# First query and output projections as three split fp32r products from one reloaded weight home

## What is computed

```python
h = layernorm(x)
q, k, v = h @ Wq, ctx @ Wk, ctx @ Wv              # 16 heads of 32
x = x + softmax(q k^T / sqrt(512 / 16), masked by len) v @ Wo
h = layernorm(x)
idx, gates = softmax_of_top2(relu(mean_over_tokens(h) @ gw1.T + gb1) @ gw2.T + gb2)   # 8 experts
proj_p(y) = y @ Wm_p.T + sum_k gates_k * ((y @ V_p[idx_k].T) * S_p[idx_k]) @ U_p[idx_k] + b_p   # rank 16
x = x + proj_o(softmax(proj_q(h) / sqrt(32) proj_k(h)^T) proj_v(h))
```

## Time and profile before

| | |
|---|---|
| median of 3 runs | 1458.2 us (1456.44 to 1459.19) |
| the profiled execution's own time | 1457.15 us |
| its span | 1455.3 us, 16992 instructions |
| TensorE busy | 1396.1 us, 96%, granted clock 0.965 |
| VectorE, ScalarE, GpSimd busy | 952.3 (65%), 862.4 (59%), 681.0 us (47%) |
| DMA | 130.81 MB, mean 90 GB/s |

### The profile page before, as it was taken

The page is one execution under the profiler, slowest core; times in us unless marked ns, Lnnn a source line. Parts: engine busy times, 40 slices in busy tenths (PEclk is TensorE's granted clock), DMA queues, the critical chain, the costliest instruction groups (busy, mean ns, idle before and its releaser), DMA issues.

```text
span 1455.3 us, 16992 instructions
## 1 busy us (share of the span) xinstructions
PE 1396.1 (96%) x5624; PEld 697.0 (48%) x5624; DVE 952.3 (65%) x1687; ACT 862.4 (59%) x1499; POOL 681.0 (47%) x411
## 2 busy tenths in 40 slices
PE   6998999999999999999999999999999999899886
PEld 4534444554455454554455554555455554444332
DVE  4364467766767677766767677766767676766632
ACT  2426364865567663866577663866577663756441
POOL 2021143546556362546556362546546362567463
PEclk9878998999999999999999999999999999999968
DMA  6533123532334224532334224531434222422210
GB/s 209 157 104 98 45 59 101 136 89 45 90 110 110 74 52 123 140 84 45 95 105 111 74 52 123 141 83 45 98 102 111 74 52 81 131 59 54 71 34 29
DMA packets 78239, 130.81 MB, mean 90 GB/s; under 512 B 26358, under 2 KB 31094, under 8 KB 75079
## 3 DMA queue, kind: packets, MB, share of 16 engines
q1 hardware_dynamic: 74055, 128.66, 33.0%
q10 hardware_dynamic: 4096, 1.06, 0.3%
HBM read 66.08 MB, written 12.21 MB: 54 GB/s over the span
## 4 chain that ended last, share of the span: by engine, by line
PE 87%; ACT 6%; issue 2%; DMA 2%; POOL 1%; DVE 1%; SPq 1%; ACTq 0%; POOLq 0%; DVEq 0%
PE pj L1091 44%; PE scT L1176 9%; PE acc L1205 8%; PE sc L1148 8%; PE sc L1137 4%; PE pj L1121 2%; PE pj L1185 2%; PE scT L1169 2%; PE pj L1193 2%; PE pj L1214 2%; PE pj L1085 2%; ACT xhat L705 2%; PE pj L1066 1%; ACT qs L788 1%; PE pj L1077 1%
## 5 line engine op out<-in xcount | busy, mean ns | idle before, releaser
L820 ACT ACTIVATE probs<-scT 128x512 f32<-128x512 f32 x512 | 289.2, 594 | 314.5 <-PE scT L1176 310.5
L936 DVE TENSOR_REDUCE negmax<-sc 128x1 f32<-128x512 f32 x512 | 338.0, 684 | 149.9 <-PE sc L1148 149.1
L683 POOL TENSOR_TENSOR probs_sum<-probs_sum,probs 128x1024 f32<-128x1024 f32 x128 | 300.0, 2368 | 61.5 <-ACT probs L820 61.5
L1148 PE MATMUL sc<-ks,qs 96*128 96x512 f32 x512 | 263.3, 549 | 6.6 <-DMA ks<-ks 3.1
L963 DVE RECIPROCAL inv_sum<-pj 128x128 f32<-128x128 f32 x256 | 224.9, 921 | 64.5 <-PE pj L1214 44.5
L1176 PE MATMUL scT<-qs,ks 99*128 99x512 f32 x512 | 254.7, 526 | 8.5 <-ACT probs L820 5.6
L1091 PE MATMUL pj<-XT,Wqk 128*128 128x512 f32 x512 | 259.6, 603 | 0.0
L679 POOL TENSOR_TENSOR probs_sum<-probs 128x1024 f32<-128x1024 f32 x64 | 151.5, 2373 | 194.2 <-ACT probs L820 194.2
L1176 PEld LDWEIGHTS scT<-qs,ks 99*128 99x128 f32 x512 | 97.2, 196 | 130.2 <-ACT probs L820 62.3
L689 POOL TENSOR_TENSOR uv_stack<-UVS_sb,uv_stack 96x1024 fp32r<-96x1024 f32 x32 | 75.7, 2364 | 171.9 <-ACT UVS_sb L727 171.9
L653 POOL TENSOR_TENSOR xhat<-xhat,inv_sum 128x128 f32<-128x128 f32 (+1 forms) x56 | 46.7, 833 | 212.6 <-DVE inv_sum L963 212.6
(11 more groups left out here) (99 smaller groups left out, 1710.1 us busy)
## 6 DMA issues: line engine op xcount, KB each, us to landing
Wqk<-in_WmT SPq DMA_DIRECT2D x16, 1024.0 KB, 6.5
Wvo<-in_WmT SPq DMA_DIRECT2D x16, 1024.0 KB, 5.7
UVS_sb<-in_UVS SPq DMA_DIRECT2D x64, 192.8 KB, 3.2
qs<-stage_lo SPq DMA_DIRECT2D x136, 64.0 KB, 2.3
qs<-qs SPq DMA_DIRECT2D x34, 256.0 KB, 3.0
X<-in_x SPq DMA_DIRECT2D x8, 1024.0 KB, 5.8
ks<-stage_lo SPq DMA_DIRECT2D x128, 64.0 KB, 2.0
ks<-ks SPq DMA_DIRECT2D x32, 256.0 KB, 3.0
```

The costliest lines, as they stand in the source:

```text
L683: nc.gpsimd.tensor_tensor(probs_sum[:, pair], probs_sum[:, pair], probs[:, kt % 2, pair], ALU.add)\
L820: nc.scalar.activation(probs[:, kt % 2, jj, :], scT[:, ST[step], :], ACT.Exp, scale=SCALE)\
L936: nc.vector.tensor_reduce(negmax[:, 0, n:n + 1], sc[:, SC[step], :], AX.X, ALU.max, negate=True)\
L1148: nc.tensor.matmul(sc[:, SC[step], :], qs[0:3 * DH, slot, jj, t * P:(t + 1) * P], ks[0:3 * DH, slot, jj, :], start=True, stop=True).then_i ...
```

## The change

1. **Split products.** Each of the 16 `q1` and 16 `out1` products of a batch becomes three products on fp32r operands that add up in the same bank: high weight x high data, high x low, low x high. `product` takes a list of terms.
2. **One home for both weights.** `W1` holds the high and low part of one 512x512 weight, 2 MB. `w1_split` makes both parts of both weights once, at the start, and stores them in DRAM (`w1_hbm`). From batch 1 on `w1_load` brings Wq's parts after the last `out1` of the batch before, and Wo's after the last `q1`.
3. **Splitting the data.** For `q1`, `xpose` of the first half writes its copy as `hi1` (ScalarE), and VectorE subtracts it from the bank into `lo1`. For `out1`, new steps `c_hi` (ScalarE) and `c_lo` (GpSimd) split each quotient of `cdivide` into the same `hi1` and `lo1`.
4. **Transposes by feature block.** An `xpose` step takes one block of 128 features from all four token tiles, not all features of one tile. The second half's step writes `XT[:, c]`; `token_sums` reduces one feature block straight into `pooled`.
5. **Room.** `STAGES` is 2. `gw1T` and the loaded U and V live in `probs1`, S in `S_sb`, and `vb` and `ob` share `bias_sb`; `gw1_load`, `vb_load` and `ob_load` bring them in every batch, on SyncE's queue, and `csT` waits until `uv_lo` has read U and V.
6. **Calendar.** The period stays; nearly all due times in `CALENDAR` and `OWN` are written anew. Between `gate_hidden` and the first `weff`, ScalarE's order is now: two exps of `sT`, `qk_split`, two exps, an `xpose` copy, `gate_scale`, a copy, an exp, two copies, two `qk_rows`, `uv_hi`; `normalize` of the next batch stands ahead of `gate_hidden`. TensorE's order there holds 14 matmuls of `sc` and `sT`, 7 `q1`, 4 `xpose`, 2 `pv`, a `den`, a `shift` and `gate_top`. `uv_lo` of the last OP pair stands ahead of the last divides, and `residual_bias` moves from a due time of 1404 to one of 2289. Column-tiled runs number 20 in a period, 162 in the kernel.

```diff
+UV_ROWS, UV_COLS = 2 * 3 * R, 2 * D
-STAGES = 3
+STAGES = 2
...
-        UVS_sb = sb("UVS_sb", [UV_ROWS, 2, UV_COLS])
+        W1 = sb("W1", [P, 2, DC, D], F32R)
+        S_sb = sb("S_sb", [UV_ROWS, 2, 4])
-        gw1T_sb = sb("gw1T_sb", [P, DC, P])
-        vb_sb = sb("vb_sb", [P, D])
-        ob_sb = sb("ob_sb", [P, D])
+        bias_sb = sb("bias_sb", [P, D])
+        lo1 = sb("lo1", [P, DC, S], F32R)
+        hi1 = sb("hi1", [P, DC, S], F32R)
...
+        gw1T_sb = probs1[:].rearrange("p j n -> p (j n)")[:, 0:D].rearrange("p (c n) -> p c n", c=DC)
+        UV_sb = probs1[0:UV_ROWS].rearrange("p j n -> p (j n)").rearrange("p (a n) -> p a n", a=2)
...
-        carrier = sb("carrier", [P, 1])
-
-
-        early = XT[:, 1].rearrange("p c n -> p (c n)")
+        carrier = sb("carrier", [P, 3])
+
+
+        early = probs[:].rearrange("p a j n -> p (a j n)")[:, DC * B * NK:DC * B * NK + 2 * P]
+        first_raw = Wqk[:, 0], ctx2T[:]
...
+                if p == QP:
+                    sp.wait_ge("w1_lo", sp.after("w1_lo", "w1_split", 0))
...
+            def w1_split(step, w):
+                sp.wait_ge("w1_hi", sp.after("w1_hi", *step))
+                sp.wait_ge("w1_lo", sp.after("w1_lo", *step))
+                queue.dma_start(w1_hbm[w], W1[:].bitcast(F32)).then_inc(sems[f"w1_stored{w}"], 16)
+
+            def w1_load(step, b, w):
+                if b == 0:
+                    return
+                if w:
+                    for i in range(DC):
+                        sp.wait_ge("pj_full", sp.after("pj_full", "q1", b, i, DC - 1))
+                else:
+                    for t in range(TT):
+                        sp.wait_ge("pj_full", sp.after("pj_full", "out1", b - 1, t, DC - 1))
+                for part in range(2):
+                    sp.wait_ge(f"w1_stored{part}", sp.after(f"w1_stored{part}", "w1_split", part))
+                queue.dma_start(W1[:].bitcast(F32), w1_hbm[w]).then_inc(sems["w1_loaded"], 16)
+
+            def gw1_load(step, b):
+                sp.wait_ge("pj_full", max(sp.after("pj_full", "cpv", b, DC - 1), sp.after("pj_full", "cden", b, DC - 1)))
+                for p in (QP, KP, VP):
+                    sp.wait_ge("uv_split", sp.after("uv_split", "uv_lo", b - 1, p))
+                queue.dma_start(gw1T_sb, gw1T.rearrange("(c p) n -> p c n", p=P)).then_inc(sems["gw1_loaded"], 16)
+
+            def vb_load(step, b):
+                sp.wait_ge("bias_added", sp.after("bias_added", "residual_bias", b - 1))
+                queue.dma_start(bias_sb[:], vb.rearrange("(a n) -> a n", a=1).to_broadcast([P, D]))\
+                     .then_inc(sems["vb_loaded"], 16)
+
+            def ob_load(step, b):
+                sp.wait_ge("pj_left_by_dve", max(sp.after("pj_left_by_dve", "v_bias", b, t) for t in range(TT)))
+                queue.dma_start(bias_sb[:], ob.rearrange("(a n) -> a n", a=1).to_broadcast([P, D]))\
+                     .then_inc(sems["ob_loaded"], 16)
+
+                if b >= 2:
+                    sp.wait_ge("uv_scaled", sp.after("uv_scaled", "uv_hi", b - 2, OP))
+                for k in range(2):
+                    rows = Ss[bass.ds(chosen[b][k], 1)].rearrange("a r p -> (a r) p")
+                    queue.dma_start(S_sb[k * 3 * R:(k + 1) * 3 * R, b % 2, :], rows).then_inc(sems["s_loaded"], 16)
+                crossed = min(b + 1, B - 1) if p == OP else b
+                sp.wait_ge("pj_full", sp.after("pj_full", "gate_hidden", crossed))
+                sp.wait_ge("pj_full", max(sp.after("pj_full", "cpv", crossed, DC - 1), sp.after("pj_full", "cden", crossed, DC - 1)))
-                    queue.dma_start(UVS_sb[k * 3 * R:(k + 1) * 3 * R, n, :], rows).then_inc(sems[f"uv_loaded{n}"], 16)
+                    queue.dma_start(UV_sb[k * 3 * R:(k + 1) * 3 * R, n, :], rows).then_inc(sems[f"uv_loaded{n}"], 16)
...
+            def c_lo(step, b, i, piece):
+                n = S // pieces(i)
+                at = slice(piece * n, (piece + 1) * n)
+                pool.wait_ge("c_hi", pool.after("c_hi", "c_hi", b, i, piece))
+                nc.gpsimd.tensor_tensor(lo1[:, i, at], ctx1T[:, i, at], hi1[:, i, at].bitcast(F32), ALU.subtract)\
+                    .then_inc(sems["c_split"], 1)
+
+            pool.walk({"c_lo": c_lo, "uv_lo": uv_lo, "deviation": deviation, "cdivide": cdivide,
...
-            def xpose(step, b, half, t):
-                if half == 0:
-                    act.wait_ge("pj_full", max(act.after("pj_full", "qk", b - 2, DC - 1, w, DC - 1) for w in range(2)))
+            def xpose(step, b, half, c):
+                if half:
+                    act.wait_ge("pj_full", max(act.after("pj_full", "v", b - 2, t, DC - 1) for t in range(TT)))
+                    act.wait_ge("pj_full", max(act.after("pj_full", "qk", b - 2, j, w, DC - 1) for j in JOBS for w in range(2)))
+                else:
+                    act.wait_ge("pj_full", max(act.after("pj_full", "out1", b - 1, t, DC - 1) for t in range(TT)))
-                nc.scalar.activation(XT[:, b % 2, :, t * P:(t + 1) * P],
-                                     pj[:, PJ[step], :].rearrange("p (c n) -> p c n", c=DC), ACT.Copy)\
-                    .then_inc(sems["pj_left_by_act"], 1)
+                dst, done = (XT[:, b % 2, c, :], "pj_left_by_act") if half else \
+                    (hi1[:, c, :], "xt_hi")
+                nc.scalar.activation(dst, pj[:, PJ[step], :], ACT.Copy).then_inc(sems[done], 1)
+
+            def w1_split(step, w):
+                act.wait_ge(("wq1_loaded", "wo1_loaded")[w], 16)
+                if w:
+                    for i in range(DC):
+                        act.wait_ge("pj_full", act.after("pj_full", "q1", 0, i, DC - 1))
+                    act.wait_ge("w1_stored0", act.after("w1_stored0", "w1_split", 0))
+                nc.scalar.activation(W1[:, 0], first_raw[w], ACT.Copy).then_inc(sems["w1_hi"], 1)
+
+            def c_hi(step, b, i, piece):
+                n = S // pieces(i)
+                at = slice(piece * n, (piece + 1) * n)
+                for k in range(DC):
+                    act.wait_ge("pj_full", act.after("pj_full", "q1", b, k, DC - 1))
+                act.wait_ge("normed", act.after("normed", "cdivide", b, i, piece))
+                nc.scalar.activation(hi1[:, i, at], ctx1T[:, i, at], ACT.Copy).then_inc(sems["c_hi"], 1)
...
+                if j == 0 and i == 0:
+                    for p in (QP, KP, VP):
+                        act.wait_ge("uv_split", act.after("uv_split", "uv_lo", b - 1, p))
+                    act.wait_ge("uv_split", act.after("uv_split", "uv_lo", b - 2, OP))
...
+            def xpose(step, b, half, c):
+                if half:
+                    return
+                for k in range(TT):
+                    dve.wait_ge("pj_full", dve.after("pj_full", "out1", b - 1, k, DC - 1))
+                dve.wait_ge("xt_hi", dve.after("xt_hi", *step))
+                nc.vector.tensor_tensor(lo1[:, c, :], pj[:, PJ[step], :], hi1[:, c, :].bitcast(F32), ALU.subtract)\
+                    .then_inc(sems["pj_left_by_dve"], 1)
+
+            def w1_split(step, w):
+                dve.wait_ge("w1_hi", dve.after("w1_hi", *step))
+                nc.vector.tensor_tensor(W1[:, 1], first_raw[w], W1[:, 0].bitcast(F32), ALU.subtract)\
+                    .then_inc(sems["w1_lo"], 1)
...
-            def token_sums(step, b, t):
-                dve.wait_ge("pj_left_by_act", dve.after("pj_left_by_act", "xpose", b, 1, t))
-                nc.vector.tensor_reduce(tile_sums[:, :, t:t + 1], XT[:, b % 2, :, t * P:(t + 1) * P], AX.X, ALU.add)\
+            def token_sums(step, b, c):
+                dve.wait_ge("pj_left_by_act", dve.after("pj_left_by_act", "xpose", b, 1, c))
+                nc.vector.tensor_reduce(pooled[:, c:c + 1], XT[:, b % 2, c, :], AX.X, ALU.add)\
-                if t == TT - 1:
-                    dve.wait_ge("gate_step", dve.after("gate_step", *step, k=1))
-                    nc.vector.tensor_reduce(pooled[:], tile_sums[:], AX.X, ALU.add).then_inc(sems["gate_step"], 1)
...
-            def xpose(step, b, half, t):
+            def xpose(step, b, half, c):
-                pe.wait_ge("xhat_done", pe.after("xhat_done", "normalize", b, half, k=t + 1))
-                for dc in range(DC):
-                    mm = nc.tensor.transpose(pj[:, p, dc * P:(dc + 1) * P], xhat[:, t, dc * P:(dc + 1) * P], ident_sb[:])
+                pe.wait_ge("xhat_done", pe.after("xhat_done", "normalize", b, half))
+                for t in range(TT):
+                    mm = nc.tensor.transpose(pj[:, p, t * P:(t + 1) * P], xhat[:, t, c * P:(c + 1) * P], ident_sb[:])
-            def product(step, name, lhsT, rhs, dc):
+            def product(step, name, terms, dc):
-                mm = nc.tensor.matmul(pj[:, p, :], lhsT, rhs, start=(dc == 0), stop=(dc == DC - 1))
+                for n, (lhsT, rhs) in enumerate(terms):
+                    mm = nc.tensor.matmul(pj[:, p, :], lhsT, rhs, start=(dc == 0 and n == 0),
```

(31 more changed lines are left out.)

279 lines of the change are left out of this document (153 added, 126 removed), and 54 rows, old and new, of tables (CALENDAR, OWN).

## The result

The changed kernel takes 1482.65 us (median of 4 runs, 1477.85 to 1485.67) against 1458.68 us, a ratio of 1.0169 with a 95% interval of 1.0136 to 1.0202. It is 1.7% slower where I forecast 0.6% faster, and outside my range.

What follows compares the result with a forecast made beforehand. The prediction took TensorE to bound the kernel. From a span of 1455.3 us, start minus 5.9, middle minus 3.6 and tail plus 1.4 gave 1447.2, forecast as a median of 1450 us, 0.6% faster, range 1428 to 1474.

Steps and rivals of the forecast that it cites:

- TensorE's work: Products fall from 0.859 to 0.705 us, minus 0.154 each; a middle stretch comes to 162.9 us against 163.5.
- The gate's times: After a batch's last out1, gate_hidden starts 14 to 16 us later and the first weff 32 to 33.5 us later.
- 3.6 us of wait on the first `weff`: At the gate: a 17.0 us chain against 13.4 us of TensorE work makes TensorE wait 3.6 us.
- my 13.4 us: TensorE work counted from gate_hidden to the first weff after the change, where 18.2 us stood.
- 0.4 and added 0.5: Allowance for waits in the rest of a middle stretch: 0.4 us taken, 0.5 in the sum.
- `STAGES` 2 ... hidden: q1_split of the next batch reuses qk_split j=3's stage; its stack DMAs are covered by uv_hi and 3 us of q1.
- The reloads, on which I spent a rival: SyncE's W1 and gw1 loads, forecast as hidden; a rival had them or the new start eat the rest, chance 0.10.
- plus 4 of a possible 8.5: Start: less TensorE cover for batch 0's gate chain and extra w1_split passes cost 4 us, bounds 0 and 8.5.
- minus 4 for `uv_lo`: Tail: uv_lo of the last OP pair moves ahead of the last divides, saving 4 us of weff's wait.
- The other three terms: Tail: plus 0.6 by step sums, plus 2.8 for the last gate, plus 2 for residual_bias moved into it.
- Of the rivals, the first: The gate waits more because gate_hidden starts over 0.7 us later than +14.8: 1474 us, chance 0.22.
- The fourth: Reloads or the new start eat the rest (gw1_load late, longer half clock in the start): 1456 to 1465 us, chance 0.10.

Runs made afterwards that it cites:

- e5_swap: Changed kernel with one due time edited, so the QP load of Wm goes ahead of the KP load: 1455.1 us, 0.9980 of the kernel before.
- e9_uv_fixed: `e5_swap` plus own homes for q1_split of blocks 0 and 1, QP's uv_hi between the two qk_rows, uv_lo behind the last psum: 1468.7 us, ratio 1.0073.
- e1_home: Changed kernel with q1_split of blocks 0 and 1 given homes of its own in xhat: 1476.5 us, ratio 1.0145.
- e4_noreload: Changed kernel without the loads of W1 from DRAM, so q1 uses the wrong weight from batch 1 on: 1482.9 us, ratio 1.0179.
- e2_loads: Changed kernel with the QP load of Wm first and the KP loads of Wm, U and V behind job 3's stack DMAs: 1512.3 us, ratio 1.038.
- e12_values: `e5_swap` with context_values 3 and 4 moved right behind batch 0's last out1: 1455.3 us, ratio 0.9995.
- e7_swap_home_uv: `e5_swap` plus own homes for q1_split of blocks 0 and 1, QP's uv_hi between the two qk_rows, uv_lo ahead of a psum: 1506.0 us, ratio 1.0341.
- e8_before_late: Kernel before with four more chained ScalarE passes of 0.71 us in QP's uv_hi of batches 1 to 7: 1484.3 us, ratio 1.018.
- e11_before_load: Kernel before with the QP load of Wm moved behind the QP loads of U and V, ahead of job 3's q stack: 1467.9 us, ratio 1.0067.

## Why the prediction was wrong

My span was 1447.2 us, the profiled one 1479.3: 32.1 us too short. By stretches: start +11.6 (253.1 for 241.5), middle +21.4 (998.8 for 977.4), tail -0.8 (227.4 for 228.2). Against `e5_swap`, where one load stands elsewhere, they are +10.1, -1.3 and -2.6. So the miss is the moved load, its waits and their clock in the middle, and the start.

- **TensorE's work: right.** 0.154 us a product, and 162.9 us for a middle stretch; `e5_swap` takes 162.6 to 162.9. The fp32r price with 128 rows, accumulating, is that of the other forms. In the changed kernel, steps of three records follow each other every 0.70 us:

```profile
452.52 0.63 PE L1211 MATMUL pj<-hi,W 128*128 128x512 f32 x2
452.99 0.39 PE L1211 MATMUL pj<-lo,W 128*128 128x512 f32 x1
453.23 0.63 PE L1211 MATMUL pj<-hi,W 128*128 128x512 f32 x2
```

These rows show 235 ns a matmul. The section "Back-to-back issue gap" of the Trainium skill, "TensorE: Matmul & The Clock Gate", which I had used, gives the 216 ns as the gap of an isolated matmul and about 131 ns for a stream of weight loads and matmuls. The trace agrees with neither.

- **The gate's times: right, its make-up wrong.** `gate_hidden` at +14.6 (14.8 forecast), the first `weff` at +32.5 (32.8). But I put 3.6 us of wait on the first `weff`, and 1.1 us are there by `e9_uv_fixed`. Of the rest, 0.65 us stand at +23, where TensorE waits for VectorE's score maxima, and 0.2 at the `q1` behind it. Most of what is left is work that my 13.4 us lacked: in `e5_swap` TensorE is busy for 14.9 of the 17.0 us between `gate_hidden` and the first `weff`. That the total came out right is two errors that cancel. (For the rest of the stretch I took 0.4 and added 0.5, which changes nothing.)
- **"`STAGES` 2 ... hidden": the step that failed first.** I put it at nothing. I named the stage, the stack DMAs and what lay between, and took 3 us of `q1` for enough without asking how long a stack takes to land from this place in the queue: 8.5 us where 3.0 was to be had. A home of its own won 10.0 us in the middle of the profiled executions (`e1_home`), under half of the middle's miss.
- **The moved load: not in the sum at all.** I counted what SyncE's queue gained (`w1_load`, `gw1_load`, S) and wrote only that `wm_load` is queued behind. That the QP load itself moves from +11 to +22, to a place ahead of the stacks and the shift rows, is in the calendar and I did not cost it. It is worth 27.6 us by the medians, of it 22.7 in the middle of the profiled executions (a miss of 21.4), and more than any term that I counted for the middle. The reloads, on which I spent a rival, cost nothing (`e4_noreload`).
- **A wait costs more than its length: not in the sum.** I priced waits in TensorE's time only. In the changed kernel's middle the waits at the second `weff` come to 13.2 us and the clock lost to 13.6. Of this, 10.2 us lie right behind these waits. The other 3.4 lie at +25 in two batches, ahead of the first `weff`, where they mostly fill its wait: it comes at +32.9 without one, and not at +32.5. So 13.2 us of waits cost 23.4. The earlier trace rows show the clock at 0.89 in start and tail, where waits are, and at 1.00 in the middle, where there are next to none; I read them as a trait of the stretches.
- **The start: term mis-sized.** I took plus 4 of a possible 8.5 for cover lost, against 9.9 us of saved products; the profiled start gives plus 15.6. The wait for `normalize`, 1.3 us before, is 6.8; other waits of the gate grew too, and 6.8 us more of clock are lost in the start (32.4 for 25.6), all of it ahead of batch 0's last `out1`. Batch 0's cross attention is a chain in both kernels: the first `out1` starts at 86.3 us before and at 87.5 after, so the products saved ahead of it bring nothing. How the 15.6 us divide into cover and clock is not shown.
- **The tail: within 0.8 us, in part by luck.** The minus 4 for `uv_lo` is there: the wait of 6.48 us is now 1.25 and 1.62. But the tail also holds the late load of the last batch, which I had at nothing:

```profile
1287.21 1.22 PE L1307 MATMUL scT<-qs,ks 99*128 99x512 f32 x2 [3.21 <-DMA qs<-shift]
```

`e5_swap` has no such wait, and its tail takes 225.6 us, 2.6 under the forecast. The other three terms were not measured singly.

Of the rivals, the first came nearest by its sign and its price (1474), but by another mechanism: `gate_hidden` was not late, and the first `weff` stood where I had it. The fourth named a longer half clock at the start, which came (until 102 us for 89), beside a start over 250 us.

## What to carry to other kernels

When an order of work is written anew, list for every DMA queue what now stands ahead of each small transfer that someone waits for; one 1 MB load in the wrong place cost 27.6 us here, and one due time won it back. I made the same mistake twice more in the experiments (`e2_loads`, `e12_values`), and once on GpSimd's queue (`e7_swap_home_uv`). A ring cut from three to two buffers needs the landing time of the transfer that frees it, taken at its new place in the queue. And in a kernel whose bound engine runs without a pause, a new pause can cost more than its length: 4.2 us and more for 2.5 in `e8_before_late`, 23.4 for 13.2 in the changed kernel's middle.

## What the runs showed that I had not expected

Not every pause brought the clock down: with 0.65 and 0.95 us nine us apart (`e5_swap`) five of six stretches lost nothing, with 0.65 to 1.6 us (`e11_before_load`) none did, with 2.5 us (`e8_before_late`) all six lost 1.7 or 3.4 us. Nor does length alone tell: in the changed kernel a wait of 1.29 us at the second `weff` lost no clock and one of 1.16 lost 1.7 us, each with 0.95 us at the first `weff` ahead of it. What decides is open. And lost clock is not always lost time: in `e5_swap` the one stretch that lost 1.7 us took 162.9 us for 162.6 or 162.7, since the loss lay ahead of a wait and filled it. The wait for one and the same bank was 0.5 us in one batch and 4.1 in another, so that one kernel shows stretches of equal work of 163.2 and 169.9 us: a single batch of such a trace would have misled in either direction.
